# A Mamba block on one core: GpSimd's C products written out of place, from a ring of 4 state tiles into a ring of 4 product tiles

## What is computed

```python
dt = softplus(dt @ dt_proj_w.T + dt_proj_b)
dA = exp(dt[..., None] * A)
dBu = (dt * h)[..., None] * Bp[:, :, None, :]
s = s * dA_t + dBu_t                      # over the rows, one after the other
y = einsum('lben,bln->ble', states, Cp)   # sum over the 16 states
y = (y + h * D) * silu(gate)
out = einsum('ble,he->blh', y, out_proj_w)
```

## Time and profile before

| what | value |
|---|---|
| median of 3 runs | 2015.46 us (2014.67 to 2020.52) |
| profiled execution, first to last instruction | 2012.5 us |
| that span below the median of the runs | 3.0 us |
| busy: DVE, POOL, PE, ACT | 1861.3, 1823.4, 1768.9, 1537.4 us |
| the same as shares of the span | 92%, 91%, 88%, 76% |
| mean granted TensorE clock | 0.969 |
| one chunk in the middle, from one of ACT's waits in `copy_y` to the same in the next | 119.34 us |

### The profile page before, as it was taken

How to read it: one execution, slowest core, us unless ns; L and a number is a source line. 1 busy time by engine, 2 the same in 40 slices (tenths; PEclk the granted TensorE clock), 3 DMA queues, 4 the chain that set the end, 5 groups by cost and what they waited for, 6 DMA issues and landing times. The chain is left out here.

```text
span 2012.5 us, 29641 instructions
## 1 busy us (share of the span) xinstructions
PE 1768.9 (88%) x9128; PEld 1316.4 (65%) x9128; DVE 1861.3 (92%) x2219; ACT 1537.4 (76%) x4897; POOL 1823.4 (91%) x757
## 2 busy tenths in 40 slices
PE   7986888989888898988989898898988889898798
PEld 5665757667576765757666675766757676575664
DVE  2798999999999999999999999999999999999995
ACT  3766778797877869778787877878787786977763
POOL 1789999999999999999999999999989999999993
PEclk9897999999999999999999999999999999999899
DMA  5655514032140412304042240403214041220300
GB/s 172 236 121 148 148 42 157 22 126 74 52 138 24 140 47 95 105 22 157 22 143 68 111 137 26 157 22 127 73 58 132 28 139 46 95 79 23 126 27 32
DMA packets 72003, 186.19 MB, mean 93 GB/s; under 512 B 6818, under 2 KB 8482, under 8 KB 63908
## 3 DMA queue, kind: packets, MB, share of 16 engines
q1 hardware_dynamic: 68148, 176.95, 25.8%
q0 software_dynamic: 3696, 7.34, 2.2%
HBM read 172.20 MB, written 12.06 MB: 92 GB/s over the span
## 5 line engine op out<-in xcount | busy, mean ns | idle before, releaser
L596 POOL TENSOR_TENSOR ub<-u,b_all 128x2048 f32<-128x2048 f32 x255 | 1167.8, 4579 | 47.1 <-DMA b_all<-bc_scratch 47.1
L752 ACT ACTIVATE decay<-dt,decay_rate 128x256 f32<-128x256 f32 (+1 forms) x2048 | 880.7, 465 | 6.0 <-DVE state_p L1503 5.4
L1503 DVE TENSOR_TENSOR_SCAN decay<-decay,carry,ub 128x512 f32<-128x512 f32 x589 | 735.5, 1275 | 11.5 <-ACT decay L752 10.5
L614 POOL TENSOR_TENSOR state_p<-state_p,c_all 128x1024 f32<-128x1024 f32 (+1 forms) x256 | 529.8, 2070 | 103.3 <-ACT carry L736 79.0
L1503 DVE TENSOR_TENSOR_SCAN state_p<-decay,carry,ub 128x512 f32<-128x512 f32 x435 | 538.3, 1269 | 38.9 <-ACT decay L752 38.4
L1070 PE MATMUL y_bank<-ident,sc_d 128*128 128x128 f32 x2356 | 351.6, 282 | 94.3 <-DVE sc_d L1518 94.3
L1518 DVE TENSOR_TENSOR sc_d<-decay,c_all 128x512 f32<-128x512 f32 x589 | 378.1, 677 | 13.1 <-PE y_bank L1070 4.4
L1070 PEld LDWEIGHTS y_bank<-ident,sc_d 128*128 128x128 f32 x2356 | 279.4, 145 | 143.3 <-DVE sc_d L1518 131.7
L1070 PE MATMUL y_bank<-ident,state_p 128*128 128x128 f32 x1740 | 247.1, 283 | 106.9 <-POOL state_p L614 105.3
L1070 PEld LDWEIGHTS y_bank<-ident,state_p 128*128 128x128 f32 x1740 | 204.2, 145 | 203.6 <-POOL state_p L614 148.0
L736 ACT ACTIVATE carry<-decay 128x2 f32<-128x2 f32 x589 | 96.4, 164 | 313.3 <-DVE sc_d L1518 313.3
(11 more groups left out here) (141 smaller groups left out, 1837.9 us busy)
## 6 DMA issues: line engine op xcount, KB each, us to landing
win_h<-win_m SPq DMA_DIRECT2D x128, 256.0 KB, 2.6
win_z<-win_m SPq DMA_DIRECT2D x128, 256.0 KB, 2.9
b_all<-bc_scratch SPq DMA_DIRECT2D x31, 1024.0 KB, 4.7
c_all<-bc_scratch SPq DMA_DIRECT2D x31, 1024.0 KB, 5.4
xa<-x SPq DMA_DIRECT2D x16, 512.0 KB, 5.1
xc<-x SPq DMA_DIRECT2D x16, 512.0 KB, 3.8
out<-xc SPq DMA_DIRECT2D x15, 512.0 KB, 3.8
ffn<-factors POOLq DMA_DIRECT2D x7, 1024.0 KB, 9.9
```

Source lines behind the costliest of these rows:

```text
L596: pool.tensor_tensor(ub[:, slot, :, :, :], u[:, (PAIRS * c + q) % U_PAIRS, :, :].unsqueeze(1).to_broadcast([P, QUAD, 2, ROWS]), b_all[:, n ...
L614: pool.tensor_tensor(part, part, c_all[:, n:n + k, :].unsqueeze(2).to_broadcast([P, k, 2, ROWS]), ALU.mult).then_inc(pooled, 1)
L752: last = act.activation(bk[:, j * ROWS + j:(j + 1) * ROWS], dt[:, pair % DT_PAIRS, j, j:], ACT.Exp, scale=decay_rate[:, e, n:n + 1])
L1503: dve.tensor_tensor_scan(dst, bk[:, :], ub[:, quad % UB_RING, i, :, :].rearrange("p j r -> p (j r)"), carried_in[:, n, 2 * q:2 * q + 1], A ...
```

## The change

POOL's product goes out of place, from `state_p` into a new tile ring `sc_p`. Both rings have 4 tiles (together the SBUF that `state_p` alone had). PE turns `sc_p`. The waits move with the data:

- POOL's product waits for the scan, and for PE to have turned the last earlier quad with the same slots (`turned_p`). It no longer waits for `carried`.
- DVE's first scan of a quad into `state_p` waits for POOL's product (`pooled`) and ACT's carry copy (`carried`) of the last earlier quad with the same slots. It no longer waits for `turned_p`.
- With 4 slots and the pattern 2, 2, 2, 1, that earlier quad is the one just before where g = 1, 5, 9 or 13, and two back in the other quads of the later chunks. (With 8 slots it was about four back.)

No instruction is added, removed or moved on any engine; only operands and waits differ. DVE has one more wait in front of one scan of each quad (two in the place of one).

```diff
-P_RING = 8
+P_RING = 4
...
-def turned_before(quad):
+def quad_before(quad):
 
     before = quad - 1
     while before >= 0 and set(slots_of(quad)).isdisjoint(slots_of(before)):
         before -= 1
-    return before + 1
+    return before
...
         state_p = sb("state_p", [P, P_RING, 2, ROWS])
+        sc_p = sb("sc_p", [P, P_RING, 2, ROWS])
...
-                last = QUAD * quad + on_pool(quad)[-1]
-                pool.wait_ge(scanned, last + 1)
-                pool.wait_ge(carried, carries_after(last))
+                pool.wait_ge(scanned, QUAD * quad + on_pool(quad)[-1] + 1)
+                wait(pool, turned_p, quad_before(quad) + 1)
                 k, slot, n = POOLED[quad], FIRST_SLOT[quad], n + on_pool(quad)[0]
-                part = state_p[:, slot:slot + k, :, :]
-                pool.tensor_tensor(part, part, c_all[:, n:n + k, :].unsqueeze(2).to_broadcast([P, k, 2, ROWS]),
+                pool.tensor_tensor(sc_p[:, slot:slot + k, :, :], state_p[:, slot:slot + k, :, :], c_all[:, n:n + k, :].unsqueeze(2).to_broadcast([P, k, 2, ROWS]),
                                    ALU.mult).then_inc(pooled, 1)
...
-                    last = turn_state(state_p[:, slot + i, :, :], False)
+                    last = turn_state(sc_p[:, slot + i, :, :], False)
...
-                        wait(dve, turned_p, turned_before(quad))
+                        before = quad_before(quad)
+                        if before >= 0:
+                            dve.wait_ge(pooled, before + 1)
+                            dve.wait_ge(carried, carries_after(QUAD * before + on_pool(before)[-1]))
```

## The result

The changed kernel took 2024.41 us (median of 5 runs, 2022.05 to 2029.05) against 2015.04 us for the kernel before (median of 5, 2013.91 to 2020.52). The ratio is 1.0044 with a 95% interval of 1.0029 to 1.0058: slower by about 0.4%, a little more than this measurement tells from no change. My 2014.0 us and my range of 2008 to 2019 us are both missed. The profiled execution has a span of 2027.3 us, 14.8 us more than before, and a mean granted TensorE clock of 0.961 against 0.969. It is the slowest of the five (2029.05 us), so its 14.8 us are more than the 9.4 between the medians.

A forecast was written before the change was run, and what follows sets the result against it. DVE was taken to set the pace, waiting only for ACT in the middle chunks. Repeating chunks 0, start -1.2, end -0.3 gave -1.5 us: span 2011.0 plus 3.0 around it, 2014.0 us; range 2008.1 to 2019.2.

The forecast's parts named there:

- The carry wait goes: POOL's product in the repeating chunks: starts 1.2 us earlier without the carry wait, none on DVE's path, 0 us.
- Twelve to thirteen repeating chunks 0: Term of the sum for the repeating middle chunks: their length does not change, 0 us.
- The loop that sets the chunk: Repeating chunks: DVE's product, nine us of PE, ACT's tanh and copies, DVE's tap set the pace; POOL isn't in it.
- Rival 1: Chain from POOL through PE and ACT to DVE is real: about 1.0 us in each of 13 chunks, 2001.0 us; chance 0.09.
- The waits that the change adds: POOL's wait for PE's turns at g = 5 and DVE's for POOL's product at g = 1, 13: 0 us expected.
- rival 3: The added semaphore wait on 255 DVE scans costs sequencer time: 2.6 us, or 20 us giving 2035.9 us; chance 0.02.
- rival 2: The tighter ring stalls DVE at g = 1 and g = 13 in 14 chunks: 15 us, 2030.5 us; chance 0.05.
- Out of place: POOL's 256 products out of place instead of in place: 11 us of POOL, 0 on the path.
- First chunks, -1.2 us: First two chunks, where POOL is late: product moves 1.4 us earlier, 1.2 expected to arrive; bounds 0 and 1.6.
- Last chunk, -0.3 us: Last chunk: DVE loses 1.1 us at g = 5, later waits may swallow it; gain 0.3, between loss 1.1 and gain 1.8.
- The time around the span: Outside the profiled span: 3.0 us added to the span of 2011.0 to give 2014.0 us.
- Slower by over 0.3%: Outcome beyond 0.3% slower than the kernel before: rivals 2 and 3 and a small part of the forecast's spread; chance 0.08.

The follow-up runs named there:

- the third: The changed kernel run unedited a third time, against the kernel before: 2027.72 us, ratio 1.0047.
- the kernel with the wait at g = 10: The changed kernel with the carry wait put back only before POOL's product of quad g = 10, against the kernel before: 2017.35 us, ratio 1.0000.
- the filler: The changed kernel with two extra expansions of dt per chunk but the last, in PE's idle stretch, against the kernel before: 2017.03 us, ratio 1.0003.
- first experiment: The changed kernel with the carry wait put back before every POOL product, against the kernel before: 2019.71 us, ratio 1.0014.

## Why the prediction was wrong, point by point

**The step that failed** is the first part, "The carry wait goes ... None of it is on DVE's path: 0 us", and with it the sum's "Twelve to thirteen repeating chunks 0". These chunks measured +14.4 us in the profiled execution, with 5 to 8 struck chunks in three executions. I followed a product that comes 1.2 us earlier to the next wait (PE then waits for DVE instead) and stopped, since a wait that only changes its name costs nothing. That takes PE's speed as a constant: the overlap that was to hide the four pairs of feed-forward matmuls and the turns behind them holds at 1.12 us for a pair and fails at 2.07. Where PE stands idle is one of the things that decides its clock, and the clock decides when the turns behind are done. The trace showed the granted clock, and I didn't read it at the places from which I moved idle time.

How the shown and the argued divide. Shown: the chunks that grow are those in which DVE waits for PE's turns; these waits follow matmuls at half the clock, over the feed-forward matmuls at the first place; filling the idle stretch there takes away the fall, the waits and the loss, and the same work behind the stretch doesn't. Not shown: why the clock falls in one chunk and not in the next, which have the same idle times. The idle sum is 2.93 us before and 2.94 after, and before has the longer single piece (2.49), so neither decides alone. That the place of the idle time matters follows from the experiments; how it does isn't known. Not shown either: what moves the fall at the other place, an estimated 5.1 of the 14.4 us in the first profile and 6.8 of 14.1 in the third (four chunks at 1.7). It came twice in the kernel with the wait at g = 10 and once in that with the filler. The Trainium skill (TensorE: Matmul & The Clock Gate, Part 1: The HAM clock gate) says that a gate passes either half of the clock's pulses or all, by how busy the array has been lately, and that the matmuls it slows differ from run to run of one kernel. The trace agrees: 0.50 and 1.00 are the levels of the windows, and six, eight and five chunks were struck in three executions of one program.

**The loop that sets the chunk** was read rightly. In the first profile's chunks without a wait for PE it is 118.78 to 119.73 us, where it was 118.83 to 119.84 before. DVE waits 0.99 us at its tap, and PE has a wait of 1.08 us for `sc_d` at 929.50 just where one was to appear. Rival 1, the chain from POOL through PE, is refuted: POOL's lead reached PE and went no further.

**The waits that the change adds** cost what I said. At g = 5 POOL's wait for the turn took the place of that for the carry; at g = 1 and 13 no scan waits for POOL. The pair of scans at 902.22, the first with the second semaphore, takes 2.45 us without a gap, as in the kernel before, so by the rows the extra reads are hidden, and rival 3 is out; so is the estimate by the Trainium skill (Advanced Engine Details and Errata, Network/Comms) of 13 to 26 us. With a late POOL (first experiment) the thin margin at g = 1 does give way, in nine chunks by up to 0.8 us: the mechanism of rival 2 exists and was covered by POOL's lead, as argued.

**Out of place** is free: the 256 products take 531.5 us where they took 529.8, and POOL in all is busy 1822.9 us, 0.5 less than before. My 11 us were a bound far off.

**First chunks, -1.2 us.** From DVE's wait at 115.29 to that at 174.38 it was 59.09 us before; after, from 114.02 to 172.43, it is 58.41, and 58.48 and 58.91 in the other two: 0.2 to 0.7 us came. The wait for PE that I meant to shorten is 1.57 us where it was 1.58. The profiled execution stands 1.8 us ahead at the tap of 340.11, but 1.3 of that it had at 114.02 already, and the second execution of the same program, at 115.33 there, had none of it. POOL's lead went into its wait for the DMA of `wo_scratch`, 2.32 us at 130.67 against 1.51, the catch I had named.

**Last chunk, -0.3 us.** From the tap of 1787.31 to the end, which is most of the last two chunks, it is 240.0 us after 237.8, so +2.2. The stall at g = 5 is there in size, on the timelines of POOL and DVE:

```profile
1922.10 2.37 POOL L613 TENSOR_TENSOR sc_p<-state_p,c_all 128x1024 f32<-128x1024 f32 x1
...
1924.56 2.46 DVE L1505 TENSOR_TENSOR_SCAN state_p<-decay,carry,ub 128x512 f32<-128x512 f32 x2 [1.12 <-ACT decay L751]
```

The row names ACT; what came last is POOL's product, which ends at 1924.47. I had 1.1 us. What should swallow it didn't: DVE waits 4.97 us for PE at the end (`yg`, line 1596) where it waited 3.3.

**The time around the span.** I took 3.0 us, the median less a span that needn't be of the same run. In all later runs, each listed with both numbers, it is 1.7 to 1.9 us. With 1.8 the same sum gives 2012.8 us and is further off.

**The rivals and the chances.** Slower by over 0.3% had 0.08 of my chances, and both mechanisms under it are not the one that came. Its time, 2024.4, lies in the gap between my range and rival 2's 2030.5. A rival "PE's idle time moves and its clock follows" could have been put in: by the durations at either clock, a half clock over four pairs of long matmuls is, as an estimate, about 1 us for each pair, 4 us, less the slack ahead of the turns, in some of 13 chunks. It measured 1.4 us in a chunk with that fall alone.

## What to carry to other kernels

Before you book an earlier product at nothing, look where the engine that consumes it will stand idle instead, and read the granted clock around that place: on TensorE moved idle time can slow the matmuls behind it, even where its sum doesn't change. When a kernel of repeating chunks gets slower, compare the chunks of one execution with each other before comparing kernels; a struck and a spared one run the same instructions. A filler in the idle stretch, with its twin placed just behind it, separates "the clock falls behind the idle time" from "more work or another order helped". Run it on the chip of the kernel that it is compared with.

## What the runs showed of the hardware

- The granted clock fell after idle stretches of 2 us (2.06 and 2.09 us), and in the kernel with the wait at g = 10 after 2.52 us. Behind the same 2 us it didn't fall in five of the twelve chunks of one execution, and fell only briefly in a sixth; nor did it fall in eleven of twelve chunks of the kernel before, with 2.49 us of waiting at nearly the same place. Which of the two happens isn't told by the length of the idle stretch.
- The kernel before has falls too, in ten of twelve chunks, where they cost nothing: 3.48 us instead of 2.00 for the convolution's matmuls. The mean granted clock, 0.969 and 0.961, tells little of the loss; where the fall lies does.
- 120 more matmuls, placed in the idle stretch, go with a ratio of 1.0003, where the changed kernel had 1.0044 to 1.0083 in other sets of runs. Placed behind it they made it slower, 1.0104 beside 1.0047 on one chip.
- One unchanged program had ratios of 1.0044, 1.0083 and 1.0047 to the kernel before on different chips or at different times, with intervals of 0.0014 to 0.0019 to either side that don't all overlap. The profiled executions had six, eight and five struck chunks, and twelve chunks took 1447.2, 1452.4 and 1446.9 us.
